# A fused transformer block: layer 1 of its local attention with the projections ahead, the value products behind, and one pair's rotary additions on VectorE

## What is computed

```python
h = shift_token(x)
qkv = h @ wqkv                              # 8 heads of 64
q, k, v = jnp.split(qkv, 3, axis=-1)
q = l2norm(q) * qs                          # t / clip(norm(t), 1e-12)
k = l2norm(k) * ksc
q, k = rotary_xpos(q, k)                    # q*cos*scale + rotate_half(q)*sin*scale
o = local_attention(q, k, v)                # windows of 64, softmax over own and previous window
x = x + o.reshape(b, n, INNER) @ wo
h = shift_token(x)
h = (h - mu) / jnp.sqrt(var + 1e-05) * lg + lb
a, g = jnp.split(h @ w1 + b1, 2, axis=-1)
x = x + (a * gelu(g)) @ w2 + b2
```

## Time and profile before

| what | value |
|---|---|
| median of 3 runs | 2047.99 us |
| the profiled execution | 2054.12 us |
| its span (first to last instruction) | 2052.3 us |
| TensorE busy | 1831.4 us, 89% |
| VectorE busy | 1322.1 us, 64% |
| ScalarE busy | 761.4 us, 37% |
| GpSimd busy | 274.9 us, 13% |
| mean granted TensorE clock | 0.950 |

### The profile page before, as it was taken

One profiled execution on the slowest core, in us unless ns is written; L12 is line 12 of the kernel. 1 busy time (PEld: TensorE's weight loads), 2 busy tenths in 40 slices (PEclk: granted clock), 3 DMA queues, 4 the chain that ended last, 5 costly groups with the idle time before them and its releaser, 6 DMA issues.

```text
span 2052.3 us, 43524 instructions
## 1 busy us (share of the span) xinstructions
PE 1831.4 (89%) x18228; PEld 1064.9 (52%) x18228; DVE 1322.1 (64%) x2768; ACT 761.4 (37%) x1442; POOL 274.9 (13%) x222
## 2 busy tenths in 40 slices
PE   6988989889898898988989889898898898988898
PEld 3655546555455544555445544556555464554644
DVE  5776557755677556775577754777547874468744
ACT  3224252343432434324433244332453333533234
POOL 2020110211101101111021010220102201022010
PEclk9999999999999999999999989999999998999989
DMA  5001100010000200002000020000200002000020
GB/s 190 8 1 19 15 6 7 2 25 9 7 7 2 31 2 6 7 2 31 2 7 7 2 32 2 12 1 3 31 3 12 1 2 31 2 7 1 3 31 8
DMA packets 27765, 29.79 MB, mean 15 GB/s; under 512 B 3684, under 2 KB 26004, under 8 KB 27156
## 3 DMA queue, kind: packets, MB, share of 16 engines
q1 hardware_dynamic: 27572, 27.01, 6.9%
HBM read 12.06 MB, written 2.36 MB: 7 GB/s over the span
## 4 chain that ended last, share of the span: by engine, by line
PE 62%; DVE 19%; ACT 8%; DMA 4%; issue 4%; SPq 3%; ACTq 0%; DVEq 0%
PE bank L986 6%; PE bank L776 5%; PE bank L1001 5%; PE bank L1011 4%; DMA phi<-parts 4%; PE bank L718 3%; PE bank L808 3%; DVE ls L1578 3%; SPq L464 3%; PE bank L866 2%; PE bank L1024 2%; ACT phi L1341 2%; ACT phi L1201 2%; ACT lc L1341 2%; PE bank L658 2%
## 5 line engine op out<-in xcount | busy, mean ns | idle before, releaser
L1743 DVE TENSOR_REDUCE amx<-bank 128x2 f32<-128x512 f32 x256 | 162.0, 685 | 77.5 <-PE bank L1024 77.5
L1307 ACT ACTIVATE silu<-bank 128x512 f32<-128x512 f32 x144 | 84.5, 596 | 290.3 <-PE bank L986 277.9
L1731 DVE TENSOR_TENSOR mh<-bank,silu 128x512 f32<-128x512 f32 x144 | 99.6, 692 | 133.7 <-PE bank L1001 131.1
L1578 DVE RECIPROCAL ls<-bank 128x256 f32<-128x256 f32 x64 | 112.2, 1753 | 61.8 <-PE bank L828 61.7
L986 PE MATMUL bank<-xn2T,w_mw 128*128 128x512 f32 x288 | 151.0, 645 | 0.0
L1011 PEld LDWEIGHTS bank<-w_mw,mh 128*128 128x128 f32 x1152 | 137.1, 192 | 25.5 <-issue 25.5
L1011 PE MATMUL bank<-w_mw,mh 128*128 128x128 f32 x1152 | 143.4, 278 | 0.0
L516 POOL TENSOR_TENSOR xB<-xn2T,lsq 128x512 f32<-128x512 f32 x32 | 40.8, 1274 | 765.1 <-ACT lsq L1313 765.1
L497 POOL TENSOR_TENSOR lc<-lc,ls 128x512 f32<-128x512 f32 x32 | 40.8, 1276 | 631.1 <-DVE lc L1531 631.1
L718 PE MATMUL bank<-hT,w_wqkv 128*128 128x512 f32 x256 | 119.1, 603 | 5.8 <-ACT hT L1281 5.7
L1563 DVE TENSOR_REDUCE lmx<-bank 128x4 f32<-128x512 f32 x128 | 79.5, 684 | 56.9 <-PE bank L776 56.9
(11 more groups left out here) (295 smaller groups left out, 3698.6 us busy)
## 6 DMA issues: line engine op xcount, KB each, us to landing
phi<-parts SPq DMA_DIRECT2D x96, 64.0 KB
lc<-parts SPq DMA_DIRECT2D x96, 64.0 KB
w_mw<-in_mw SPq DMA_DIRECT2D x3, 1152.0 KB
x_in<-in_x SPq DMA_DIRECT2D x8, 256.0 KB, 2.8
out<-res SPq DMA_DIRECT2D x8, 256.0 KB, 2.3
w_wqkv<-in_wqkv SPq DMA_DIRECT2D x2, 768.0 KB, 6.4
w_w<-in_w SPq DMA_DIRECT2D x1, 682.0 KB, 4.2
mh<-in_rotary SPq DMA_DIRECT2D x1, 512.0 KB, 6.0
```

The source lines that it names most:

```text
L1307: A(silu[:, n % 2, :], bank_of("moe_g", n)[:], ACT.Silu).then_inc(sem["moe_silu"], 1)
L1578: V.reciprocal(lrec[:, k % 2, :], bank_of("loc_den", k)[:, 0:SEQ]).then_inc(sem["loc_rec"], 1)
L1731: V.tensor_tensor(mh[:, n % 4, :], bank_of("moe_u", n)[:], silu[:, n % 2, :], ALU.mult).then_inc(sem["moe_h"], 1)
L1743: V.tensor_reduce(amx[:, 2 * b:2 * b + 2, h], bank_of("att_max", n)[:].rearrange("p (t k) -> p t k", t=2), AX.X, ALU.max).then_inc(sem["at ...
```

## The change

All of it is in layer 1; layer 0 keeps its order.

- TensorE: the eight raw products stand together, `sums(0)` follows the eighth instead of the sixth. `values(0)` stands between `sums(1)` and the columns, `values(1)` and `values(2)` behind the columns, `values(3)` behind the transposition of the roots. The `job` calls follow, so banks and waits change too.
- ScalarE copies the values 0 to 2 after the sums, the last one after `lrT`.
- GpSimd leaves out the last pair; its subtraction and addition are done by VectorE, after the third pair's scaling and ahead of the last one. `loc_rot` counts 14 in a turn instead of 16.
- VectorE does `favor_out(0)` after the scaling of the second pair, not ahead of the roots.

```diff
-    "loc_rot": 16, ...
+    "loc_rot": 14, ...
...
-                if l == 1 and c == 5:
-                    job("loc_v", TT, "loc_v", TT + 1)
...
-            for j in range(1 if l else EARLY, TT - 1):
+            for j in range(0 if l else EARLY, 1 if l else TT - 1):
                 job("loc_v", TT * l + j, "loc_v", TT * l + j + 1)
             job("loc_sum", l, "loc_sum", l + 1)
-            job("loc_v", TT * l + TT - 1, "loc_v", TT * l + TT)
+            if l:
+                for j in (1, 2):
+                    job("loc_v", TT * l + j, "loc_v", TT * l + j + 1)
...
             job("loc_rT", l, "loc_rT", l + 1)
+            if l:
+                job("loc_v", TT * l + TT - 1, "loc_v", TT * l + TT)
...
-                    for p, (qk, g) in enumerate(PAIRS):
+                    for p, (qk, g) in enumerate(PAIRS[0:3] if l else PAIRS):
...
-                        if p == 2:
-                            if l:
-                                values(0)
+                        if p == (3 if l else 2):
                             sums(0)
...
-                    if l:
-                        values(1)
                     favor_heads(l, "raws")
                     sums(1)
                     if l:
-                        values(2)
+                        values(0)
...
                     last.then_inc(sem["loc_sum_ps"], 1)
-                    values(3)
+                    if l == 0:
+                        values(3)
+                    if l:
+                        values(1)
+                        values(2)
                     favor_heads(l, "sums")
...
                     last.then_inc(sem["loc_rT_ps"], 1)
+                    if l:
+                        values(3)
...
-                    if l:
-                        favor_out(0)
...
                         m = 4 * l + p
+                        if m == 7:
+                            V.tensor_tensor(lc[:, 6, :], lc[:, 6, :], lsb[2], ALU.subtract)
+                            link(V.tensor_tensor(lc[:, 7, :], lc[:, 7, :], lsb[3], ALU.add))
                         dve.wait_ge(sem["loc_rb_ps"], now("loc_rb_ps", m + 1))
...
                         favor_heads(l, "rb", p)
+                        if l and p == 1:
+                            favor_out(0)
```

More of the change, by code:

```diff
@@ L60 @@
     "vec_step": 1, "route_d": 1, "moe_base": 1,
-    "loc_rot": 16, "favor_done": 1, "favor_rec": 2, "att_rest": 1, "att_part3": 1, "moe_xw": 8,
+    "loc_rot": 14, "favor_done": 1, "favor_rec": 2, "att_rest": 1, "att_part3": 1, "moe_xw": 8,
     "stack_in": 26 * 16, "nm_out": 16, "nm_in": 32,
@@ L311, in build @@
             favor_jobs(l, "raws")
-            for j in range(1 if l else EARLY, TT - 1):
+            for j in range(0 if l else EARLY, 1 if l else TT - 1):
                 job("loc_v", TT * l + j, "loc_v", TT * l + j + 1)
             job("loc_sum", l, "loc_sum", l + 1)
-            job("loc_v", TT * l + TT - 1, "loc_v", TT * l + TT)
+            if l:
+                for j in (1, 2):
+                    job("loc_v", TT * l + j, "loc_v", TT * l + j + 1)
+            if l == 0:
+                job("loc_v", TT - 1, "loc_v", TT)
             favor_jobs(l, "sums")
             job("loc_rT", l, "loc_rT", l + 1)
+            if l:
+                job("loc_v", TT * l + TT - 1, "loc_v", TT * l + TT)
             favor_jobs(l, "rT")
@@ L1210, in _ @@
                         A(sq8[c], bank_of("loc_raw", n)[:], ACT.Square).then_inc(sem["loc_sq"], 1)
-                        if l == 1 and c == 5:
-                            local_value(0)
                         if l == 0 and c == 1:
@@ L1219, in _ @@
                     A(lsq[:, 0, :], bank_of("loc_ss", l)[:], ACT.Copy).then_inc(sem["loc_ss"], 1)
-                    for j in range(1 if l else EARLY, TT):
+                    for j in range(0 if l else EARLY, TT - 1 if l else TT):
                         local_value(j)
@@ L1227, in _ @@
                     A(lrT[:], bank_of("loc_rT", l)[0:48, 0:256].bitcast(BF16), ACT.Copy).then_inc(sem["loc_rT"], 1)
+                    if l:
+                        local_value(TT - 1)
                     def favor_total():
@@ L1553, in _ @@
                         m = 4 * l + p
+                        if m == 7:
+                            V.tensor_tensor(lc[:, 6, :], lc[:, 6, :], lsb[2], ALU.subtract)
+                            link(V.tensor_tensor(lc[:, 7, :], lc[:, 7, :], lsb[3], ALU.add))
                         dve.wait_ge(sem["loc_rb_ps"], now("loc_rb_ps", m + 1))
                         for c in (4 * qk + 2 * g, 4 * qk + 2 * g + 1):
-                            dve.wait_ge(sem["loc_rot"], now("loc_rot", 2 * m + c % 2 + 1))
+                            if m < 7:
+                                dve.wait_ge(sem["loc_rot"], now("loc_rot", 2 * m + c % 2 + 1))
                             V.tensor_tensor(lc[:, c, :], lc[:, c, :], bank_of("loc_rb", m)[:], ALU.mult).then_inc(sem["loc_qk"], 1)
                         favor_heads(l, "rb", p)
+                        if l and p == 1:
+                            favor_out(0)
                     for g in range(2):
```

## The result

| what | before | changed |
|---|---|---|
| median of 20 runs each | 2049.39 us (2042.33 to 2057.99) | 2033.71 us (2023.25 to 2046.27) |
| the profiled execution | 2054.12 us | 2027.67 us |
| its span | 2052.3 us | 2025.9 us |
| mean granted TensorE clock | 0.950 | 0.960 |
| TensorE busy | 1831.4 us | 1811.1 us |

The changed kernel takes 0.9916 of the time before, 95% interval 0.99 to 0.9933. That is 17.2 us less of 2049.39 (13.7 to 20.5). The prediction said 2029 us, range 2015 to 2042, faster: it holds in direction and range. The profiled execution gained more, 26.4 us.

A forecast was written before the change was run, and what follows sets the result against it. Bound: TensorE (busy 89%) and the chain feeding it, in layer 1 through VectorE's roots. Per turn 1.9 + 1.05 - 0.2 = 2.75, + 0.6 - 1.0 = 2.35 us; 18.8 in eight turns, so 2029 us, range 2015 to 2042.

The forecast's parts named there:

- Sums earlier: Layer 1, ahead of the roots: second square sums directly follow the first, so the columns come 1.9 us earlier per turn.
- The collision: Start of layer 1's roots: first root operation no longer waits for GpSimd, 0.21 to 0.25 us instead of 1.29; gain 1.05.
- Rival 3: At the roots: GpSimd's third pair holds the first root operation, or last value product costs 0.86; 2038 us, chance 0.14.
- The last value product: On TensorE between transposition and spreading: the product partly delays the spreading, costing 0.2 us a turn (bounds 0 to 0.86).
- S: Start of VectorE's scaling in layer 1, after the masking; predicted 2.75 us earlier per turn.
- Three operations in VectorE's queue: Between scaling and maxima: `favor_out(0)`, subtraction and addition add 0.61, 0.61 and about 0.7 us; VectorE reaches maxima at S + 6.8.
- The clock: First scores keep 2.4 GHz, gaining 0.6 us; second scores' clock falls in half the turns, 2.0 us each, -1.0 average.
- the new hole: TensorE's wait ahead of the second scores, until the third maximum ends: estimated 0.9 us busy in 3.6.
- The sum: All terms per turn: 2.75 + 0.6 - 1.0 = 2.35 us, 18.8 us in eight turns.
- Rival 1: Ahead of the second scores: the clock stays up in the new hole, 26.8 us gained, 2021 us; chance 0.2.
- Rival 2: Clock still falls ahead of the first scores, second scores run at 2.4 GHz; 22 us gained, 2026 us; chance 0.1.

The follow-up runs named there:

- the order alone: Kernel before with only the new order of TensorE products and ScalarE copies; GpSimd keeps the last pair, `favor_out(0)` stays ahead of the roots: ratio 1.0008, median 2051.28 us.

## Why the prediction was right, point by point

- Sums earlier, 1.9 us: 2.05 (12.93 to 10.88). The two limits that I found equal are equal: the columns end 0.04 us ahead of the roots, as before, and VectorE comes to them from its rotary products at the same moment.
- The collision, 1.05: 1.09 in this turn (1.29 to 0.20), the mean over both layers 0.754 to 0.208. But the wording of the risk was too small: "at worst all of it" took the collision for one operation of GpSimd. Had the pair stayed, two would have been hit, with a fall of the clock behind them. The term had no room: I put GpSimd's end at 1127.47 and the first root operation at 1127.45. GpSimd's addition ended 0.16 us behind that operation's start, and it cost nothing, since the operation needs 0.20 by itself. Rival 3's mechanism did not occur.
- The last value product, -0.2: nothing that can be seen, since 2.05 and 1.09 make the whole of what S moved. The product's row shows 1.08 us. The first spread product starts 1.46 us behind the masking (1122.62 against 1121.16) where it was 1.30, so the delay of 0.2 is there; but VectorE is through with the masking only at 1123.05, and it is hidden. The experiment that puts it back prices the placing at +0.40 us. Together the scaling comes 3.13 us earlier on average (19.06 to 15.93), where 2.75 was predicted.
- Three operations in VectorE's queue: maxima at S + 6.8 predicted, S + 6.72 measured; the third maximum's end at S + 8.7, and the mask product that waits for it starts at S + 8.65 (1131.70 - 1123.05). The bound did move to VectorE, and of the 2.2 us that I put the clock's gift at 0.51 arrived on average (7.23 to 6.72; 0.68 in the fifth turn), where 0.6 was predicted.
- The clock: the first scores kept it in eight of eight turns, as predicted. TensorE did 2.83 us in the 3.60 of the roots, where I had 2.5 or more. But the reason that I gave, busier roots, isn't enough: with the value product back ahead of the roots TensorE did 2.92 us in them and the clock fell in all eight turns, and with `favor_out(0)` back it did 2.00 and the first scores kept the clock in seven. That the order also filled the wait behind the transposition was not in my working. In the new hole it fell in seven of eight, where half was predicted, but a fall cost 1.45 us and not 2.0, as the low stretch was 3.4 us and not up to 6.8. The product is -1.27 a turn against -1.0. Two errors of opposite sign, and here the prediction was right partly by their cancelling. The row behind the price belongs to the old hole, in which TensorE did 0.38 us of matmuls in 3.60; in the new one it did 1.22 in 3.00, and the low stretches were half as long.
- The sum, 2.35 us a turn: 2.38 measured (3.13 + 0.51 - 1.27, rounded). The range had some 6 us for the other stretches' clock; the profiled pair has 7.4 us beyond this stretch, and the ratio none. One slip has no weight: one to eight falls at 2.0 us give 2023 to 2037 us, not 2021 to 2037.
- Rival 1, the clock kept in the new hole, didn't come: it fell in seven turns with 1.22 us of matmuls in the three microseconds before the second scores, where the kernels with 1.65 and 2.77 us in the same place kept it. My reading of the Trainium skill ("TensorE: Matmul & The Clock Gate", Part 1), that some matmuls in the hole keep the clock up, is contradicted by these seven falls. The page isn't: beside the idle array it describes a kernel whose array idles only briefly between groups of matmuls and whose clock goes back and forth between the two levels. Rival 2's number, 2026 us, was measured on another kernel, where its mechanism was made to act.
- What I had not asked: whether the hole could be avoided. I set the three operations against 2.54 us of idleness, in which they had room, and priced the fall. They cost more than that: with all three elsewhere the maxima start at S + 5.22, 1.50 us sooner than in the change. Other places for them, where VectorE or GpSimd waits anyway, saved 34 us more by the ratio (51.0 against 17.2), twice what the change itself did.

## What to carry to other kernels

Price a reordering together with what it is pulled into: here the earlier roots alone gained nothing, since they ran into GpSimd's whole pair, and the pair's move alone gained 12.3 us, while both together gained 27.8 before a third part took 10.6 away. Side work goes where its engine waits in the new schedule, and not into the queue of the engine that feeds TensorE: it may be hidden there, and still open a hole that costs the clock, and the clock then falls where nothing hides it. When the clock falls in a hole, make it shorter first; one operation of 0.6 us less went with no fall instead of seven, in two kernels.

## What the runs showed of the hardware

- VectorE operations of only 128x64, with both inputs in SBUF, last as long as GpSimd's operation of 128x512 beside them: 1.21 and 1.19 us instead of 0.23. The Trainium skill ("GPSIMD Engine Reference", 1. Specifications) says that GpSimd shares its SBUF interfaces with VectorE, and that it contends with VectorE's instructions of two SBUF inputs and with those in a 2-port performance mode; for two SBUF inputs the rows agree. Operations with one input in PSUM weren't held (1.94 us for four maskings beside GpSimd, as without it). The first root operation has one input, of int32, and was held too: 1.29 us where it started 0.03 us behind GpSimd's, 1.01 where 0.96 us of GpSimd's were left (the order alone). No row shows in which mode it ran. Where only 0.12 or 0.16 us of GpSimd's operation were left it took its 0.20.
- It goes the other way as well: GpSimd's subtraction took 1.72 us instead of 1.27 beside `favor_out(0)`, which had started first.
- In all eleven profiles a low stretch was 3.4, 6.8 or 10.2 us long, but for the last one of each execution, and its price depends on the place: none for 3.4 us where VectorE's queue covers it, 1.45 us in the second scores. In the roots it took the last value product from 1.08 to 2.02 us.
- Still open: the 7 us of the profiled pair beyond the stretch, the 5 to 10 us of the best kernels, and why the eighth turn of the change kept the clock. The same treatment of layer 0, whose clock fell in four of eight turns, wasn't tried.
